# Edge keys of a graph kernel fetched in 13 blocks of 113 to 128 rows instead of 12 of 128 and one of 32

## What is computed

```python
h = jnp.maximum(_layernorm(x, axis=-1), 0.0)
x = x + _L0_gnn_ref(h, src, dst, ...)      # attention over the edges, 10 heads of 13
h = jnp.maximum(_layernorm(x, axis=-1), 0.0)
x = x + _L1_gnn_ref(h, src, dst, ...)      # four graph convolutions
...
ft = (layer_norm(h) @ W_att).reshape(n, 10, 13)                    # in _L0_gnn_ref
scores = jnp.einsum('ehd,ehd->eh', ft[src], ft[dst]) / jnp.sqrt(13)
a = softmax of scores over the edges that share a dst
agg = jax.ops.segment_sum(ft[src] * a[:, :, None], dst, num_segments=n)
...
out = jax.ops.segment_sum(h[s] * norm[:, None], d, num_segments=n)  # in every convolution
```

## Time and profile before

| | us |
|---|---|
| median of 3 runs | 3985.91 |
| lowest and highest run | 3983.66, 3988.76 |
| span of the profiled execution | 3987.6 |
| prelude, to the first gather of the attention stage | 117.3 |
| from the first to the last of the 1568 gathers | 1959.9 |
| convolutions, about | 1727 |

### The profile page before, as it was taken

One profiled execution on the slowest core, in us unless ns is written; L12 is line 12 of the kernel. 1 busy time (PEld: TensorE's weight loads), 2 busy tenths in 40 slices (PEclk: granted clock), 3 DMA queues, 4 the chain that ended last, 5 costly groups with the idle time before them and its releaser, 6 DMA issues. The chain is left out here.

```text
span 3987.6 us, 61840 instructions
## 1 busy us (share of the span) xinstructions
PE 3679.6 (92%) x21902; PEld 2157.9 (54%) x21902; DVE 2167.3 (54%) x3396; ACT 1880.8 (47%) x5147; POOL 1505.2 (38%) x1605
## 2 busy tenths in 40 slices
PE   5899999999999999999985879999999999999999
PEld 3566666666666666666653544445444544454444
DVE  8788888888888888888874750002100210012000
ACT  4788888888888888888863660002000100011000
POOL 2677777777777777777760000000000000000000
PEclk8788888888888888888886989999999999999999
DMA  6443333333333333333334126665666566665665
GB/s 202 128 109 104 105 106 105 105 106 105 106 105 105 106 106 106 105 106 105 105 92 88 38 65 204 204 196 181 199 194 208 174 194 203 205 189 184 213 204 159
DMA packets 467250, 560.45 MB, mean 141 GB/s; under 512 B 45449, under 2 KB 411684, under 8 KB 466686
## 3 DMA queue, kind: packets, MB, share of 16 engines
q1 hardware_dynamic: 383558, 366.63, 30.4%
q0 software_dynamic: 51168, 107.68, 12.2%
q10 hardware_dynamic: 32248, 82.62, 5.6%
HBM read 455.16 MB, written 103.20 MB: 140 GB/s over the span
## 5 line engine op out<-in xcount | busy, mean ns | idle before, releaser
L900 POOL DMA_INDIRECT fts<-ft_tab,src_all x1568 | 1483.0, 946 | 478.0 <-issue 477.4
L2171 PE MATMUL cv_acc<-cv_cnt,cv_parts 128*128 128x512 bf16 (+1 forms) x7056 | 1431.3, 366 | 0.0
L2171 PEld LDWEIGHTS cv_acc<-cv_cnt,cv_parts 128*128 128x128 bf16 x7056 | 666.0, 98 | 761.7
L2006 DVE TENSOR_TENSOR cv_y<-cv_acc,dis_row 128x512 f32<-128x512 f32 (+1 forms) x52 | 34.4, 661 | 1355.1 <-PE cv_acc L2171 1326.5
L937 DVE TENSOR_TENSOR ohk<-iota_ps,key_cols 128x784 bf16<-128x784 f32 x784 | 724.9, 966 | 6.1
L1030 ACT ACTIVATE dist_l<-lo_iota,low 128x128 bf16<-128x128 f16 x1960 | 593.7, 388 | 18.6 <-ACT low L1025 0.8
L1189 PE MATMUL agg_ps<-terms,oh 128*64 128x141 f32 x2744 | 528.7, 364 | 25.6 <-DVE terms L974 25.0
L1189 PEld LDWEIGHTS agg_ps<-terms,oh 128*64 128x64 f32 x2744 | 458.1, 180 | 80.6 <-DVE terms L974 67.3
L1082 ACT CAST strip<-adj_ps 128x392 bf16<-128x392 f32 x784 | 372.2, 475 | 271.4 <-PE adj_ps L1133 239.2
L1133 PE MATMUL adj_ps<-ohk,ohl 128*128 128x196 bf16 x3136 | 431.2, 263 | 0.0
L951 DVE TENSOR_TENSOR prod<-ftd_ps,fts 128x780 f32<-128x780 f32 (+1 forms) x392 | 271.1, 692 | 220.5 <-DMA fts<-ft_tab,src_all 212.3
(11 more groups left out here) (261 smaller groups left out, 2919.9 us busy)
## 6 DMA issues: line engine op xcount, KB each, us to landing
cv_cnt<-adj SPq DMA_DIRECT2D x96, 2048.0 KB, 8.3
cv_cnt<-adj SPq DMA_DIRECT2D x48, 2176.0 KB, 8.6
adj<-strip ACTq DMA_DIRECT2D x196, 392.0 KB
fts<-ft_tab,src_all POOLq DMA_INDIRECT x1568
win<-ft_tab SPq DMA_DIRECT2D x196, 65.0 KB
agg_tab<-res SPq DMA_DIRECT2D x196, 35.2 KB
cv_cnt<-adj SPq DMA_DIRECT2D x8, 512.0 KB, 3.7
agg_tab<-zero_f SPq DMA_DIRECT2D x10, 352.5 KB
```

What stands on the lines that cost most here:

```text
L900: nc.gpsimd.indirect_dma_start(fts[u][:, k, :], None, ft_tab[:, :], bass.IndirectOffsetOnAxis(src_all[:, n, k:k + 1], 0)).then_inc(gathere ...
L2171: last = nc.tensor.matmul(a[:, 0:width], parts[:, r, b, :], cnt[q][:, 0:width // SUB, (b - b0) * SUB:(b - b0 + 1) * SUB], start=(b == 0 an ...
```

## The change

`FETCH` holds the row counts of 13 blocks, `FETCH_AT` the running sums. The sum of the counts is still 1568. The places are converted by one instruction over 128 rows and 13 columns where two were, so POOL waits for a count of 1. The writes into `key_cols` and `low_cols` start at the block's first strip, which is no longer always a multiple of eight. Nothing outside `prelude` differs.

```diff
-BLOCKS = -(-NH // P)
+FETCH = (128, 127, 126, 125, 124, 122, 121, 120, 118, 116, 114, 113, 114)
+FETCH_AT = (0,) + tuple(accumulate(FETCH))
+BLOCKS = len(FETCH)
+assert FETCH_AT[-1] == NH and max(FETCH) <= P
...
-        in_block = lambda b: min(P, NH - b * P)
+        in_block = lambda b: FETCH[b]
...
-            pool.wait_ge(s["start_at_made"], 2)
+            pool.wait_ge(s["start_at_made"], 1)
...
-                to = key_cols[:, b * P // NA:(b * P + m) // NA].rearrange("p g a c -> p c (g a)")
+                to = key_cols[:].rearrange("p g a c -> p c (g a)")[:, :, FETCH_AT[b]:FETCH_AT[b] + m]
...
-                nc.vector.scalar_tensor_tensor(to, turned_keys, -float(KSTEP * P * b),
+                nc.vector.scalar_tensor_tensor(to, turned_keys, -float(KSTEP * FETCH_AT[b]),
...
-                nc.vector.tensor_scalar(start_at[:, 0:BLOCKS - 1], cnt_ps[:, 0:BLOCKS - 1], 2.0 * COARSE, None, ALU.mult
+                nc.vector.tensor_scalar(start_at[:], cnt_ps[:, 0:BLOCKS], 2.0 * COARSE, None, ALU.mult
                                         ).then_inc(s["start_at_made"], 1)
-                nc.vector.tensor_scalar(start_at[0:NH % P, BLOCKS - 1:], cnt_ps[0:NH % P, BLOCKS - 1:BLOCKS], 2.0 * COARSE,
-                                        None, ALU.mult).then_inc(s["start_at_made"], 1)
...
-                to = low_cols[:, b * P // NA:(b * P + m) // NA].rearrange("p g a c -> p c (g a)")
+                to = low_cols[:].rearrange("p g a c -> p c (g a)")[:, :, FETCH_AT[b]:FETCH_AT[b] + m]
...
-                last = nc.tensor.matmul(cnt_ps[0:m, b:b + 1], start_f[0:1, b * P:b * P + m], ones[0:1, 0:1],
+                last = nc.tensor.matmul(cnt_ps[0:m, b:b + 1], start_f[0:1, FETCH_AT[b]:FETCH_AT[b] + m], ones[0:1, 0:1],
```

More of the change, by code:

```diff
@@ L4 @@
 from contextlib import ExitStack
+from itertools import accumulate
 F32 = mybir.dt.float32
```

## The result

The changed kernel takes **3996.15 us** in the median of 7 runs (3994.06 to 4000.61) where the kernel before, run beside it, takes 3985.91 (3983.66 to 3989.68): a ratio of 1.0027, 95% interval 1.0018 to 1.0037, or 10.2 us more. The forecast was 3985.8, no change, with 3995 as the upper end of the range. What happened is the first rival, the fetch on one DMA engine.

What follows compares the result with a forecast made beforehand. POOL's unbroken issue of 1568 gathers was taken to bound the attention stage, and a chain the prelude's end. Terms of -0.07, -0.14 and +0.14 gave -0.1 us after rounding: 3985.91 - 0.1 = 3985.8, range 3979 to 3995.

Steps and rivals of the forecast that it cites:

- the first rival: Prelude, block 1: 127 rows go through one DMA engine and land late; +8 to +11 us, 3994 to 3997; chance 0.12.
- "I take 0" for the fetches: Prelude: 13 fetches of the same 1568 rows, issued before needed, cost 0; the last one's longer POOL work is hidden.
- 1.8 us of cover: Block 1 in the prelude: its landing can be 1.8 us late before DVE's key_cols at 61.42 is delayed.
- blocks 5 and 11 stay covered: Prelude, first rival: fetches of 122 rows (6.3 us) and 113 rows (11.6 us) are issued two cycles ahead, so hidden.
- a written rule: Trainium skill's DMA page: 127 partitions use one engine; its exception, some direct POOL-path copies, uses all 16, count divided rounding up.
- The small terms: Prelude: -0.07 for L470, -0.14 for shorter early cycles, +0.14 for ACT's last copy; -0.1 us after rounding.
- DVE's statistics after the places: Prelude, places: one DVE instruction, L470, goes and gives DVE back 0.07 us; gain at most 0.07 us.
- said was +0.14: Prelude's end: ACT's last column copy takes 0.14 us more, moving nf_hnT from 107.42 to 107.56 and the last store with it.
- the layout costs nothing: Prelude, PSUM offsets at odd multiples of 4 bytes: taken as 0, upper bound 2.5 us on DVE, about the same on ACT.
- POOL's work on the last fetch: Prelude's last fetch: a 114-row block costs POOL at most 0.07 us more than the 32-row one, hidden before the barrier.
- The pace of the gathers: Attention stage: unequal fetches change POOL's time per gather, 1.57 us per nanosecond; 3976 or 3994; chance 0.07, 0.05 for faster.
- The last gather: Attention stage's end: another queue place could remove the last gather's delay (used 4.3 us after issue), 1.8 us, 3984; chance 0.10.

Runs made afterwards that it cites:

- the repaired kernel: The changed kernel, but block 1's fetch brings 128 rows of which 127 are used (the spare row): 3990.51 us, ratio 1.0002.
- the kernels in sixteens: The changed kernel with seven blocks of 128 rows, then six of 112, all multiples of 16: 3986.01 us, ratio 1.0002.
- its second execution: The kernel before, unchanged, run again for a second trace: 3983.76 us.
- the reordered counts: The changed kernel with the same 13 row counts in another order, 127 and 113 rows as blocks 10 and 11: 3988.13 us, ratio 1.0007.
- the 126-row kernel: The changed kernel with another table: block 1 has 126 rows, the last block 34, all others 128: +2.2 us against the kernel before, ratio 1.0005.

## Why the prediction was wrong

**The step that failed** is "I take 0" for the fetches. It priced a 127-row fetch by the rows of 128 and 32, the only counts in the trace of before. Both are multiples of 16, so the earlier trace rows could tell nothing of the odd ones, and I still took the value at which the edit costs nothing. Its true price is 11 us on the prelude: landing 15.4 us in place of 3.6, less 1.8 us of cover, and about one more.

**The rival had the mechanism, the place and, with some luck, the sum.** It gave landing at 71.0, PE turned the block at 70.18; `key_cols` at 72.3, it was 71.34; 8 to 11 us on the time, it was 10.2; 3994 to 3997, it was 3996.15. The luck is in the rate. Its 19.9 GB/s was a mean over a stretch in which all sorts of transfers ran; alone, one engine moved 25. At 25 GB/s, an estimate, the 127 rows take 10.4 us, which leaves 5.0 for the rest of the landing, where the rival had 13.1 and 3.0. The two errors nearly cancel. The rival named DVE's order as what passes the loss on, and that held. It said that blocks 5 and 11 stay covered: in the repaired kernel PE waits for neither. What was wrong is its **chance of 0.12**. Against it I had set that the 32-row block landed among the others, which is no evidence, as 32 is 16 x 2 and would do so under either rule. What was left was a written rule that spoke for the loss, an exception to it that was for another kind of copy, and no row against it. That is at least an even chance. The range, with its upper end put just inside the rival's 3994 to 3997, was cut too short for the same reason.

**The small terms held, but for one.** The start of DVE's statistics after the places went from 0.15 to 0.09 us, -0.06 where -0.07 was said. At the end of the prelude, the counterpart of the earlier trace rows:

```profile
117.74 0.40 ACT L640 COPY low_cols<-keys_ps 128x228 f32<-128x228 f32 x1
...
117.98 0.70 ACT L625 ACTIVATE nf_hnT<-nf_T_ps,nf_lnb,nf_lnw 128x384 f32<-128x384 f32 x1
118.78 1.80 PE L707 MATMUL nf_ft_ps<-w_att,nf_hnT 128*128 128x130 f32 x14 [1.23 <-ACT nf_hnT L625]
```

ACT hands over 0.24 us after the copy's start and not 0.11: +0.13, said was +0.14, on the path as said. The columns at odd offsets take DVE 0.42 us for 254 numbers, beside 0.41 for 256 before: the layout costs nothing, as taken. Their sum, about 0, is what the kernels in sixteens and with the spare row show. The one that failed is POOL's work on the last fetch: 114 rows were to take at most 0.07 us more than 32, and took 1.11 us against 0.88. It was hidden, as said.

**The pace of the gathers** differs by 2.4 ns from start to start, in two values with nothing between. But the kernel before shows both, 947 ns in the earlier trace rows and 944 in its second execution. Of the others, the reordered counts and the 126-row kernel ran at 947, the rest at 944, so both chips show both. A rival that I had tied to the change thus lives in the execution. It can hide or feign 3.7 us in one profile, and did: it is why the profiled span grew by 7.0 where the medians grew by 10.2.

**The last gather** was used 4.45 us after its issue, 4.3 before, and 4.1 to 4.6 in the other kernels. That rival fell: row counts don't touch it.

## What to carry over

Before the row count of an indirect DMA is changed, look at its divisors: here a count's largest divisor up to 16 set how many engines carried it, and 127 rows took four times as long as 128. Where the count can't be chosen, fetch a spare row and don't use it, or place the odd count where the program issues it cycles ahead of need; it is the first fetches, with an in-order engine waiting behind them, that pay. And where the profile has no row for a case while a written rule speaks against the edit, "0, by the nearest row" is not the likeliest value unless that row could have shown the effect.

## What was not expected of the hardware

- **POOL works longer when fewer engines are used.** One fetch of about the same size took POOL 0.95 us at 128 rows, 1.01 at 126, 1.21 at 125, 1.69 at 122 and 2.57 at 127. For a kernel whose bound is POOL's issue, a bad count would cost this on each one, even if every landing were hidden.
- **A fetch behind a one-engine fetch is late with it.** In the changed kernel the fetches of 126 and 125 rows behind block 1 landed after 12.7 and 13.4 us, and in the repaired one after 4.5 and 5.6. In the kernel with block 1 at 127 rows and the next ten at 128, the three plain fetches behind it took 13.4, 12.8 and 12.2, where the same three take 3.4 to 4.2 in the kernel before. A 128-row fetch goes to all 16 engines by the divisor rule, the busy one among them. The windows fit: in the changed kernel only one engine's worth was moving from 66.5 to 69.5 us, with four fetches open, and they landed at 70.1 (block 1), 70.3, 72.3 and 72.4. No run tested it apart.
- **A long piece of POOL's work can hold up DVE.** Besides the 1889 ns above, in the repaired kernel a small DVE instruction (`centre`, 98x2) took 585 ns, where before it takes 158, and ended at 84.95 when POOL's work on its 113 rows ended at 84.98; in the changed kernel it took 295 and ended at 95.25, POOL at 95.28. Other DVE instructions beside the same work, the `key_cols` among them, kept their length. Which are held, and by what, no run isolates.
- **Two paces of one loop.** The 1568 gathers run at 1.2484 or at 1.2507 to 1.2509 us from start to start, by execution, which is worth 3.7 us in any profile of this kernel. What sets it is open.
